# PSUM of an attention stage divided anew: four score banks and three transpose banks, with copies and value product placed again

## The reference

```
h = relu(layernorm(x)); qkv = h @ W            # 4 heads of 32
scores = q @ k.T / sqrt(32) + mask             # 512 x 512 for each head
attn   = softmax(scores)
x      = x + attn @ v
```

## Time and profile before

| | us |
|---|---|
| median of 3 runs | 688.59 (686.69 to 688.61) |
| the profiled execution | 685.76 |
| its span, first to last instruction | 684.0 |
| of it before the attention stage | 407.8 |
| attention stage | 276.2 |
| PE, DVE, ACT busy, whole span | 646.0, 481.2, 398.9 |

### The profile page before, as it was taken

The page is one execution under the profiler, slowest core; times in us unless marked ns, Lnnn a source line. Parts: engine busy times, 40 slices in busy tenths (PEclk is TensorE's granted clock), DMA queues, the critical chain, the costliest instruction groups (busy, mean ns, idle before and its releaser), DMA issues.

```text
span 684.0 us, 13068 instructions
## 1 busy us (share of the span) xinstructions
PE 646.0 (94%) x3737; PEld 501.9 (73%) x3737; DVE 481.2 (70%) x1331; ACT 398.9 (58%) x923; POOL 130.6 (19%) x112
## 2 busy tenths in 40 slices
PE   6999999999899998999999778999999999999996
PEld 4767997789778897788987656666666666666663
DVE  6662563377833777336653569999999999999993
ACT  3433232124541345412232559999999999999994
POOL 5110235012330133301133910000000000000001
PEclk8999999999999999999999999999999999999999
DMA  3101110211235111350037896677777777777710
GB/s 111 32 0 47 32 31 16 72 40 60 75 150 170 42 58 74 147 173 13 25 109 218 181 409 191 149 180 172 175 173 177 174 176 171 177 176 177 183 58 32
DMA packets 48656, 82.53 MB, mean 121 GB/s; under 512 B 5104, under 2 KB 13680, under 8 KB 48496
## 3 DMA queue, kind: packets, MB, share of 16 engines
q1 hardware_dynamic: 48192, 82.07, 44.8%
q10 hardware_dynamic: 432, 0.07, 0.1%
HBM read 52.76 MB, written 29.36 MB: 120 GB/s over the span
## 4 chain that ended last, share of the span: by engine, by line
PE 30%; issue 20%; ACT 4%; POOL 4%; DVE 2%; POOLq 0%; DVEq 0%; ACTq 0%
PE ps_t L1517 13%; PE ps_o L1548 7%; PE ps_s L1532 7%; ACT v L1467 1%; ACT p_t L1458 1%; POOL z_l L831 1%; POOL h L715 1%; PE ps_o L1555 1%; POOL v L824 1%; DVE v L1489 1%; ACT ut L896 0%; DVE low L1489 0%; DVE p_t L1483 0%; PE ps_u L95 0%; PE ps_u L97 0%
## 5 line engine op out<-in xcount | busy, mean ns | idle before, releaser
L1467 ACT ACTIVATE v<-v,low 128x512 f32<-128x512 f32 x256 | 182.4, 716 | 7.0 <-DVE low L1489 6.7
L1489 DVE CUSTOM_DVE_ANT_0 v<-ps_s,pL 128x512 f32<-128x512 f32 x256 | 165.6, 685 | 11.8 <-PE ps_s L1532 11.1
L1517 PE MATMUL ps_t<-ident,v 128*128 128x128 f32 x1024 | 155.0, 274 | 4.8 <-ACT p_t L1458 4.2
L1517 PEld LDWEIGHTS ps_t<-ident,v 128*128 128x128 f32 x1024 | 123.2, 140 | 33.1 <-DVE p_t L1483 8.8
L1532 PE MATMUL ps_s<-pL,pH 128*128 128x512 f32 x256 | 122.8, 481 | 2.3 <-DVE low L1489 2.0
L1483 DVE COPY p_t<-ps_t 128x512 f32<-128x512 f32 x128 | 85.0, 685 | 0.9 <-PE ps_t L1517 0.9
L1458 ACT ACTIVATE p_t<-ps_t 128x512 f32<-128x512 f32 x128 | 74.4, 583 | 0.3 <-PE ps_t L1517 0.3
L1445 POOL TENSOR_TENSOR o_n<-o_n,x 128x512 f32<-128x512 f32 x16 | 20.6, 1286 | 265.6 <-DVE o_n L1499 265.6
L1532 PEld LDWEIGHTS ps_s<-pL,pH 128*128 128x128 f32 x256 | 48.3, 189 | 30.4 <-DVE low L1489 17.4
L95 PE MATMUL ps_v<-rH,ut 128*128 128x384 f32 x192 | 65.1, 339 | 4.6 <-DVE v L1083 4.6
L1548 PE MATMUL ps_o<-p_t,v_sb 128*32 128x512 f32 x512 | 61.4, 597 | 4.6 <-issue 3.6
(11 more groups left out here) (208 smaller groups left out, 1102.0 us busy)
## 6 DMA issues: line engine op xcount, KB each, us to landing
pH<-qk_dram SPq DMA_DIRECT2D x64, 256.0 KB, 6.8
pL<-qk_dram SPq DMA_DIRECT2D x64, 256.0 KB, 7.6
qk_dram<-qk SPq DMA_DIRECT2D x12, 512.0 KB, 3.3
x_ln<-in_x SPq DMA_DIRECT2D x16, 256.0 KB, 3.1
x_res<-in_x SPq DMA_DIRECT2D x16, 256.0 KB, 2.6
x_dram<-v SPq DMA_DIRECT2D x16, 256.0 KB, 3.1
v_sb<-v_dram SPq DMA_DIRECT2D x16, 256.0 KB, 9.3
x<-x_dram SPq DMA_DIRECT2D x16, 256.0 KB, 9.4
```

Of the source, the lines that this page charges most:

```text
L1467: act.activation(s_ring[:, n % RING, :], s_ring[:, n % RING, :], ACT.Exp, bias=low[:, n:n + 1], scale=-1.0, accum_out=lsum[par][:, n:n + 1 ...
L1489: dve.tensor_tensor_reduce(s_ring[:, n % RING, :], ps_s[S_BANK[n]][:, :], mask[:, n // HEADS, :], -SCALE, 3.0e38, ALU.add, ALU.min, low[:, ...
L1517: mm = pe.transpose(ps_t[n % T_BANKS][:, j * 128:(j + 1) * 128], s_ring[:, n % RING, j * 128:(j + 1) * 128], ident[:, :])
```

## The change

The attention stage gets four score banks and three transpose banks. All that follows from it is placed again:

- S(n) waits for r(n-4) in place of r(n-3).
- T(n) waits for the copy three tiles back in place of four, but tile 15 is put in bank 1: T(15) waits for c(13), T(0) for c(12), T(1) for c(15), T(2) for c(14), each of the batch before.
- Nine copies are ACT's and seven DVE's (eight and eight before).
- Copies by slot after: on ACT c(0) in 5, c(2) in 7, c(4) in 9, c(6) in 11, c(7) in 12, c(10) in 15, c(11) in 0', c(12) in 1', c(15) in 4'; on DVE c(1) in 6, c(3) in 9, c(5) in 11, c(8) and c(9) in 14, c(13) and c(14) in 4'.
- The value product is 4 matmuls in slot 7, 4 in slot 8 and 8 in slot 14 (8 and 8 in slots 7 and 14 before).

```diff
-    T_BANKS = 4
-    COPIER = "DDADADADDAAADADA"
+    T_BANKS = 3
+    COPIER = "ADADADAADDAAADDA"
...
-    COPY_AFTER = [2, 1, 1, 1, 0, 2, 0, 3, 2, 1, 1, 1, 2, 0, 2, 0]
+    COPY_AFTER = [0, 0, 0, 1, 0, 1, 0, 0, 1, 0, 0, 0, 0, 2, 1, 0]
...
-    PV_AT = {7: 8, 14: 8}
+    PV_AT = {7: 4, 8: 4, 14: 8}
...
-    S_BANKS = 3
-    S_BANK = [n % S_BANKS for n in range(TILES - 1)] + [1]
-
-    S_BACK = [next(k for k in range(1, TILES) if S_BANK[n - k] == S_BANK[n]) for n in range(TILES)]
+    S_BANKS = 4
+    assert TILES % S_BANKS == 0
+    S_BANK = [n % S_BANKS for n in range(TILES)]
+    T_BANK = [n % T_BANKS for n in range(TILES - 1)] + [1]
+
+    T_BACK = [next(k for k in range(1, TILES) if T_BANK[n - k] == T_BANK[n]) for n in range(TILES)]
...
-        src = ps_t[m % T_BANKS][:, :].rearrange("p (j i) -> p j i", j=T)
+        src = ps_t[T_BANK[m]][:, :].rearrange("p (j i) -> p j i", j=T)
...
-                s, value = copied(n - T_BANKS, b) if n >= T_BANKS else copied(n - T_BANKS + TILES, b - 1)
+                s, value = copied(n - T_BACK[n], b) if n >= T_BACK[n] else copied(n - T_BACK[n] + TILES, b - 1)
...
-                mm = pe.transpose(ps_t[n % T_BANKS][:, j * 128:(j + 1) * 128],
+                mm = pe.transpose(ps_t[T_BANK[n]][:, j * 128:(j + 1) * 128],
...
-                    wait(pe, s_max, TILES * b + n - S_BACK[n] + 1)
+                    wait(pe, s_max, TILES * b + n - S_BANKS + 1)
```

## The result

| | before | after |
|---|---|---|
| median, us | 688.43 | 699.25 |
| range of the runs | 686.69 to 688.61 | 697.69 to 701.68 |
| profiled execution: time, span | 685.76, 684.0 | 701.68, 699.9 |
| start of the attention stage in it | 407.9 | 411.8 |
| OT to OT, mean of 14 | 16.59 | 17.37 |

The change makes the kernel slower, ratio 1.0166, 95% interval 1.0131 to 1.0201, 10.8 us between the medians. 706.1 was forecast: the direction is right, the time lies in the range, the loss is 10.8 us in place of 17.5. The first 4 us of the span's difference lie ahead of the stage, where nothing was changed; they look like scatter, since the first OT of the other runs' profiles lies anywhere from 438.4 to 443.4. The stage itself went from 276.2 to 288.1 us.

What follows compares the result with a forecast made beforehand. Bound taken: a once-per-batch chain from second value product to T(15), then along PE. Terms +1.04 +0.20 -0.14 +0.25 -0.17 = +1.18 us, times 14, plus 1.0, gave 706.1 us; range 695.0 to 711.5.

Steps and rivals of the forecast that it cites:

- What bounds the kernel before: A chain closing once per batch: second value product to T(15), 6.64 us, then PE to the next one, 10.18.
- Part one: Second value product to T(15), which waits for c(13) behind four reductions on DVE: 7.68 against 6.64, +1.04 us a batch.
- Part two: T(15) to T(1'), which waits for c(15) in ACT's queue: 1.57 against 1.37, +0.20 us a batch.
- Part three: Placing around the first value product: T(1) to T(2) -0.14, the cut product +0.25, T(4) to T(9) -0.17 us.
- T(2) to PV, 1.00 "I keep": Step on PE from T(2) to the first value product, kept at 1.00 us; up to 0.4 may go.
- Part four: One more copy on ACT is covered, 0.48 us if not; the fourth score bank costs nothing and gains nothing.
- The sum: All terms together: +1.18 us a batch, 16.5 over 14 batches, +17.5 us in total.
- Ahead of the first OT: Start of the attention stage, where ACT has 14 copies instead of 11: +1.0 us, between 0 and 2.
- tail: After the last batch, T(15) waits for c(13) on DVE instead of c(11) on ACT: 0, with 0.4 either way.
- A: Rival, chance 0.10: transposes do not hold PE and four score banks end DVE's waits for scores; 685 us.
- B: Rival, chance 0.06: slower by ACT's extra copy alone, +0.48 us a batch, 695.3 us.
- C: Rival, chance 0.04: the banks change but the placings cancel, +0.0 to 2 us, 689 us.

Runs made afterwards that it cites:

- e7: Kernel before with the reciprocal of the row sums moved ahead of r(8) on DVE; 685.83 us, ratio 0.9969.
- e6: Kernel before with copy c(11) moved ahead of e(0') on ACT; 685.18 us, ratio 0.9958.
- e2: Changed kernel with copy c(13) two slots earlier on DVE, slot 2' in place of 4'; 699.5 us, ratio 1.0179 to the kernel before.
- e4: Changed kernel's copies and value product with the old banks, three for scores and four for transposes; 687.62 us, ratio 1.000 to the kernel before.
- e12: Changed kernel with tile 15 in transpose bank 0 in place of bank 1; 720.74 us, ratio 1.0458 to the kernel before.

## Why the prediction was right, and where its sum was off

**What bounds the kernel before: wrong in its second half.** The leg from the second value product to r(0') and e(0') was right (e7 and e6 shorten it and pay). From there the prediction followed T(15) and PE; the runs show ACT's copies up to c(15) and the wait of PV for it.

Along that chain the loss adds up. In the two batches shown, before and after: r(0') to c(15) 4.54 and 4.05; c(15) to the first PV 0.87 and 1.89; first PV to the second 6.95 and 7.08; second PV to the next r(0') 4.46 and 4.47. The batch is 0.67 longer. In the shorter kind c(15) to PV was 0.68 before, and the batch is 0.87 longer; the mean is 0.78. So the new placing brings c(15) half a microsecond forward, and having three transpose banks in place of four takes back more than twice that, because the wait for c(15) now stands at T(1'), with S(7') and T(2') between it and PV.

**Part one, +1.04 from the second value product to T(15): right in size, wrong as a price.** 7.68 was summed, 7.66 measured (526.96 to 534.62). But e2 takes that hold away and wins nothing. What it had to be compared with was not T(15) before but the later of two chains at T(1'). That the way by T(15) is only 0.1 us shorter than the one by c(15), so that its sum is a fair measure of the loss, is luck.

**Part two, +0.20 from T(15) to T(1'): right in its path, +0.12 in size.** 1.57 summed, 1.49 measured; c(15) is ACT's own 0.86 behind T(15), as counted (0.85), and only c(15) to T(1') was 0.63 for 0.72. This is the link that binds; the prediction gave it the small end of the sum. Its path, r(0') to c(15) 4.07, was measured as 4.05 (531.43 to 535.48).

**Part three.** T(1') to T(2') 0.72 summed, 0.73 measured. **T(2) to PV, 1.00 "I keep", is the term that failed**: 0.53 measured. In the kernel before it was the wait for c(15); after, c(15) starts 1.36 us ahead of T(2'), because T(1') has already waited for it. The same wait is paid once in either kernel, and the sum had charged it twice in the changed one. Against the mean of 0.81 and 1.00 that is 0.37 us, times 14 over 5 us; the working allowed "up to 0.4" for it, for another reason. First PV to T(4) 3.11 summed, 3.20 measured (T(3) to PV is 0.52, for which 0.45 was put, within the bound of +0.39 that it gave); T(4) to T(9) 3.33 and 3.35; T(9) to PV 0.59 and 0.53.

**Part four: right.** One copy more on ACT is covered (e4: 1.000). No run has a fourth score bank without giving up a transpose bank for it, so what it wins by itself isn't shown; DVE's waits for scores did not fall. The Trainium skill's page "Perfetto Trace Analysis", § Optimizing Tensor Performance, asks for matmul groups to rotate through different banks; e4 and the changed kernel differ in nothing but how seven banks are divided, and the one with more of them for the matmuls is 11.6 us slower. The Trainium skill's page "Perfetto Trace Analysis", § Optimization Strategy, says that one and the same gap, repeated on the engine that should be full, can mean too few PSUM buffers; by that rule, the trace agrees: PE's gap of 1.20 to 1.34 at T(15) in each batch is a bank short (e4, with the fourth, has none there), though e2 shows that filling this gap alone wins nothing.

**The sum.** +1.18 a batch forecast, +0.78 measured; 0.37 of the difference is that one term. Ahead of the first OT +1.0 forecast, +1.1 measured (29.9 to 31.0 from the start of the stage); tail 0 and -0.1.

**The rivals.** A asked for T(15) at 6.7 us or less: it came at 7.66. But e2 shows that A's point of decision was the wrong one: with T(15) free the time is the same. B would have been OT to OT 17.07 and a time of 695.3; e4, with the ninth copy and without the banks, denies it. C is out.

## What to carry to other kernels

A ring of buffers that feeds two engines in turn sets a deadline for each reader: with one bank fewer each copy is due one tile sooner, and here what bounded was the copy that stood deepest in its engine's queue, not the one under which the longest wait was listed. Before a wait is priced, look for a second chain that ends at the same place; take the wait away (as e2 does) before believing it. And a gap on PE that a profile calls "issue", in front of an instruction with several waits, is to be compared with the starts of all that it waits for: here PV's start 0.68 or 0.87 behind one copy, by kind of batch, named it, while its distance from the T ahead of it changed from run to run.

## What the runs showed of the hardware

In e12 PE is held 1.70 us at T(0') in batch after batch. In some batches the granted clock falls right behind the hold, in others not. The busy times of three stretches of e12, the last within the second; columns: stretch, length, PE, PEld, DVE, ACT, POOL busy, then the granted clock, DMA share and GB/s:

```profile
524.50:529.50 5.00, 3.30 (x26) 1.97 (x24) 3.91 (x12) 4.26 (x13) 0.00 (x0) 1.00 1.03 209
...
544.80:549.40 4.60, 4.55 (x23) 2.70 (x23) 2.23 (x7) 3.24 (x9) 0.00 (x0) 0.63 1.07 213
546.00:548.00 2.00, 2.00 (x9) 1.49 (x8) 1.17 (x2) 0.84 (x3) 0.00 (x0) 0.50 1.09 209
```

and PE's rows at the two holds:

```profile
526.70 0.66 PE L1519 MATMUL ps_t<-ident,v 128*128 128x128 f32 x4 [1.70 <-ACT p_t L1460]
...
544.85 0.66 PE L1519 MATMUL ps_t<-ident,v 128*128 128x128 f32 x4 [1.70 <-ACT p_t L1460]
```

Both holds are as long, and behind the second the clock averages 0.63 of full speed for 4.6 us; from 546 to 548 it is 0.50 throughout, 1.2 GHz in place of 2.4. The batch with the drop is 19.74 us long (538.35 to 558.09); the one of its kind without is 18.16 (462.96 to 481.12). Over 430 to 690 e12's granted clock is 0.95; in the changed kernel, with holds of up to 1.3 us, it is 1.00 over 430 to 680. So behind holds that were lengthened from about 1.2 to 1.7 us, 8 of 14 batches lost another 1.6 us each by the clock, more than the 0.67 that the later wait costs. That the hold's length brings on the drop is argued, as no run changed it alone, and what decides between batches isn't shown.

Two links cost 0.2 us more in every second batch of the kernel before: c(15) to PV is 0.68 and 0.87 in two neighbouring batches, and OT to r(0') is 1.63 and 1.82. The changed kernel has only the second of them, and its two kinds differ by 0.2 in place of 0.4. The loop takes two batches a turn; which of its instructions costs this was not tested.
